# Flamingo block with a selective scan and a top-2 factorised FFN: delta times u moved from GpSimd to VectorE, with smaller edits to the gates

## The reference

```python
x_ = einsum('ed,bld->bel', in_proj_w, ctx)              # 512 channels
u = silu(conv4(x_) + conv_b)
dt_lo, Bm, Cm = split(einsum('ke,bel->bkl', x_proj_w, u))
delta = softplus(dt_proj_w @ dt_lo + dt_proj_b)
for t in range(512):                                    # 16 states for each channel
    state = state * exp(delta[t] * A) + (delta[t] * u[t]) * B[t]
    y[t] = sum_n state * C[t]
x = x + tanh(g_xattn) * (y + D * u) * silu(layernorm(x))
h = layernorm(x)
sc = h @ Wr.T; idx = top_k(sc, 2)
g = softmax(sc) * one_hot(idx); g = g / (g.sum() + 1e-8)
out = einsum('bts,btsr,srh->bth', g, h @ U, V)
gate = g @ sigmoid(attr @ Wa)
x = x + tanh(g_ffn) * out * (0.9 + 0.2 * gate)
```

## Time and profile before

| what | value |
|---|---|
| three runs | 554.56, 556.52, 556.17 us, median 556.17 |
| profiled execution | 554.37 us, its span 552.6 us |
| mean granted TensorE clock in it | 0.978 of full |
| DMA | 37.82 MB, mean 68 GB/s |
| length of the phases in it | phase 0 29.4, 1 and 2 24, 3 and 4 29, 5 to 11 28 to 34, 12 to 18 about 19, 19 13 us |
| before phase 0, after phase 19 | 32.3 us, 26.3 us |

### The profile page before, as it was taken

How to read it: one execution, slowest core, us unless ns; L and a number is a source line. 1 busy time by engine, 2 the same in 40 slices (tenths; PEclk the granted TensorE clock), 3 DMA queues, 4 the chain that set the end, 5 groups by cost and what they waited for, 6 DMA issues and landing times.

```text
span 552.6 us, 9388 instructions
## 1 busy us (share of the span) xinstructions
PE 502.3 (91%) x3154; PEld 381.2 (69%) x3154; DVE 459.9 (83%) x844; ACT 395.3 (72%) x704; POOL 479.3 (87%) x359
## 2 busy tenths in 40 slices
PE   6668989898798899999999999999899999999788
PEld 2156979767677687759687887678667756676654
DVE  2878999969899989779899999787878878977952
ACT  3369687758776787577968787578789778777632
POOL 0169999999999999989999999989999999988920
PEclk9877999999989999999999999999999999999899
DMA  4793000127320001046220000066100000000001
GB/s 109 258 351 142 2 2 0 39 54 240 131 77 2 0 1 58 0 159 211 77 95 2 20 1 21 6 226 222 49 20 1 21 20 21 1 20 21 0 21 38
DMA packets 18274, 37.82 MB, mean 68 GB/s; under 512 B 5537, under 2 KB 6305, under 8 KB 18226
## 3 DMA queue, kind: packets, MB, share of 16 engines
q1 hardware_dynamic: 18226, 37.22, 20.3%
HBM read 32.75 MB, written 4.46 MB: 67 GB/s over the span
## 4 chain that ended last, share of the span: by engine, by line
PE 52%; POOL 15%; ACT 13%; DVE 10%; issue 8%; DMA 1%; DVEq 0%; ACTq 0%; SPq 0%; POOLq 0%
PE p_s L718 14%; PE p_y L740 12%; POOL state L541 8%; PE p_v L773 5%; PE p_f L764 5%; DVE state L1197 4%; POOL dbu L526 4%; PE p_tr L684 4%; ACT da L960 3%; PE p_pr L647 3%; DVE x L1145 2%; PE p_pr L640 2%; ACT p_s L960 2%; ACT L912 2%; ACT L960 1%
## 5 line engine op out<-in xcount | busy, mean ns | idle before, releaser
L541 POOL TENSOR_TENSOR state<-state,c_bc 128x1024 f32<-128x1024 f32 (+1 forms) x158 | 304.5, 1940 | 14.0 <-DVE state L1197 11.2
L1197 DVE TENSOR_TENSOR_SCAN state<-da,p_s 128x512 f32<-128x512 f32 (+1 forms) x158 | 172.7, 1104 | 28.7 <-PE p_s L718 27.3
L718 PEld LDWEIGHTS p_s<-pair_b,du_t 128*128 128x128 f32 x1264 | 163.9, 196 | 36.1 <-issue 22.6
L718 PE MATMUL p_s<-pair_b,du_t 128*128 128x128 f32 x1264 | 178.9, 283 | 4.0 <-DVE state L1197 2.5
L740 PE MATMUL p_y<-ident,state 128*128 128x128 f32 x1024 | 150.4, 275 | 0.8 <-POOL state L541 0.8
L960 ACT ACTIVATE da<-delta,a_neg 128x512 f32<-128x512 f32 (+1 forms) x190 | 119.2, 642 | 25.2 <-DVE state L1197 24.7
L740 PEld LDWEIGHTS p_y<-ident,state 128*128 128x128 f32 x1024 | 120.6, 142 | 20.2 <-issue 15.3
L526 POOL TENSOR_TENSOR dbu<-du,pair_b 128x1024 f32<-128x1024 f32 (+1 forms) x64 | 116.5, 1820 | 4.7 <-DMA pair_b<-bc_rows 4.7
L1197 DVE TENSOR_TENSOR_SCAN state<-p_s,dbu 128x512 f32<-128x512 f32 (+1 forms) x98 | 101.1, 1037 | 5.5 <-POOL dbu L526 4.5
L960 ACT ACTIVATE p_s<-delta,a_neg 128x512 f32<-128x512 f32 (+1 forms) x130 | 74.9, 580 | 39.4 <-DVE state L1197 38.7
L764 PE MATMUL p_f<-u_sb,h_t 128*128 128x512 f32 x112 | 55.2, 595 | 1.5 <-DVE gw L1298 1.5
(11 more groups left out here) (178 smaller groups left out, 612.9 us busy)
## 6 DMA issues: line engine op xcount, KB each, us to landing
c_bc<-bc_rows SPq DMA_DIRECT2D x32, 512.0 KB, 5.6
pair_b<-bc_rows SPq DMA_DIRECT2D x13, 512.0 KB, 6.4
xs<-in_x SPq DMA_DIRECT2D x16, 256.0 KB, 4.3
out<-ot SPq DMA_DIRECT2D x14, 256.0 KB, 2.0
cx<-in_ctx_t SPq DMA_DIRECT2D x4, 512.0 KB, 3.6
u_sb<-in_u_w SPq DMA_DIRECT2D x1, 1024.0 KB, 7.9
v_sb<-in_v_w SPq DMA_DIRECT2D x1, 1024.0 KB, 14.6
w_in<-in_in_w_t SPq DMA_DIRECT2D x1, 384.0 KB, 4.5
```

The lines of the kernel that those rows point to most:

```text
L541: eng.tensor_tensor(pair, pair, c_bc[:, 2 * p:2 * p + 2, c0:c0 + w], ALU.mult).then_inc(po_cs, 1)
L718: mm = eng.matmul(p_s[g % BANKS][:, t * P:(t + 1) * P], du_t[:, f % 2, t, :], diagonals_of(n // 2)[:, n % 2, c0 // P + t, :], start=(t == ...
L1197: eng.tensor_tensor_scan(slot(g)[:, 0:w], decayed, added, first, ALU.mult, ALU.add).then_inc(ve_scan, 1)
```

## The change

`du` gets two buffers and is made by DVE for all phases: for phase f+1 after scan 9 of phase f, behind `gate_y(f - 1, 1)`. POOL no longer makes it. The waits of all readers become one on `ve_du`. The ring of `u` has five places in place of six. The casts of the two best indices go; the comparisons read the uint32 index as their scalar. In the gates, `0.2 * tanh(g_ffn)` is folded into `aw` and `0.9 * tanh(g_ffn)` into `gf` once, in phase 0, and one tiny operation of each tile goes.

```diff
-U_RING = 6
+U_RING = 5
-        du = sb("du", [P, L])
+        du = sb("du", [P, 2, L])
-        top_f = sb("top_f", [P, Q, 2])
-        GOPS = 9
-        def wait_for_du(eng, f):
-            if f:
-                eng.wait_ge(po_du, f)
-            else:
-                eng.wait_ge(ve_du, 1)
+        GOPS = 8
...
-            def times_u(f):
-                b, k, c0, w = PHASE[f]
-                eng.wait_ge(ve_dl, f + 1)
-                eng.wait_ge(pe_turn, TURN["du", f - 1] + 1)
-                eng.wait_ge(po_dbu, by_pool[f, pool_pairs(b)[0]])
-                if f == 1:
-                    eng.wait_ge(ve_dbu, 2)
-                eng.tensor_tensor(du[:, 0:w], delta[:, f % 2, 0:w], u[:, (Q * b + k) % U_RING, c0:c0 + w],
-                                  ALU.mult).then_inc(po_du, 1)
...
                 if p == pool_pairs(b)[0]:
-                    wait_for_du(eng, f)
-                eng.tensor_tensor(dbu[:, i % 2, :, 0:w], du[:, 0:w].unsqueeze(1).to_broadcast([P, 2, w]),
+                    eng.wait_ge(ve_du, f + 1)
+                eng.tensor_tensor(dbu[:, i % 2, :, 0:w], du[:, f % 2, 0:w].unsqueeze(1).to_broadcast([P, 2, w]),
                                   rows_of_b(p)[:, :, c0:c0 + w], ALU.mult).then_inc(po_dbu, 1)
...
-                early_u = k == 0 and c0 == 0
-                if early_u and not many:
-                    times_u(f + 1)
                 times_c(f, 3)
                 if many:
                     times_b(f, pairs[3])
-                if f < LAST and not (early_u and not many):
-                    times_u(f + 1)
                 times_c(f, 4)
...
             def turn_du(f):
-                wait_for_du(eng, f)
-                turn("du", f, du[:, :], PHASE[f][3] // P)
+                eng.wait_ge(ve_du, f + 1)
+                turn("du", f, du[:, f % 2, :], PHASE[f][3] // P)
...
             def exp_scores(T):
-                eng.wait_ge(ve_top, 4 * T + 4)
+                eng.wait_ge(ve_top, 3 * T + 3)
...
+            def times_u(f):
+                b, k, c0, w = PHASE[f]
+                eng.wait_ge(ve_dl, f + 1)
+                if f >= 2:
+                    eng.wait_ge(pe_turn, TURN["du", f - 2] + 1)
+                    eng.wait_ge(po_dbu, by_pool[f - 1, pool_pairs(PHASE[f - 1][0])[0]])
+                eng.tensor_tensor(du[:, f % 2, 0:w], delta[:, f % 2, 0:w], u[:, (Q * b + k) % U_RING, c0:c0 + w],
+                                  ALU.mult).then_inc(ve_du, 1)
...
-                else:
-                    eng.wait_ge(ve_top, 4 * T + 3)
-                    eng.tensor_copy(top_f[:, i, 0:1], top_i[:, i, 0:1])
-                    eng.tensor_copy(top_f[:, i, 1:2], top_i[:, i, 1:2]).then_inc(ve_top, 1)
...
-                    eng.scalar_tensor_tensor(out=e1, in0=iota_f[:, :], scalar=top_f[:, i, 0:1], in1=ex,
+                    eng.scalar_tensor_tensor(out=e1, in0=iota_f[:, :], scalar=top_i[:, i, 0:1], in1=ex,
                                              op0=ALU.is_equal, op1=ALU.mult).then_inc(ve_g, 1)
-                    eng.scalar_tensor_tensor(out=e2[:, i, :], in0=iota_f[:, :], scalar=top_f[:, i, 1:2], in1=ex,
+                    eng.scalar_tensor_tensor(out=e2[:, i, :], in0=iota_f[:, :], scalar=top_i[:, i, 1:2], in1=ex,
                                              op0=ALU.is_equal, op1=ALU.mult).then_inc(ve_g, 1)
...
                 elif part == 3:
                     made(6)
-                    eng.tensor_scalar(a[:, 4:5], a[:, 3:4], a[:, 2:3], 0.2, ALU.mult, ALU.mult).then_inc(ve_g, 1)
-                elif part == 4:
+                    eng.tensor_scalar(a[:, 4:5], a[:, 3:4], a[:, 2:3], gf[:, :], ALU.mult, ALU.add).then_inc(ve_g, 1)
+                else:
                     made(7)
-                    eng.tensor_scalar(a[:, 5:6], a[:, 4:5], 0.9, a[:, 2:3], ALU.add, ALU.mult).then_inc(ve_g, 1)
-                else:
-                    made(8)
-                    eng.tensor_scalar(gw[:, i, :], em, a[:, 5:6], gf[:, :], ALU.mult, ALU.mult).then_inc(ve_g, 1)
+                    eng.tensor_scalar(gw[:, i, :], em, a[:, 4:5], a[:, 2:3], ALU.mult, ALU.mult).then_inc(ve_g, 1)
...
                         eng.reciprocal(aw[:, :], aw[:, :]).then_inc(ve_k, 1)
                         eng.wait_ge(ve_k, 6)
+                        eng.tensor_scalar(aw[:, :], aw[:, :], gf[:, :], 0.2, ALU.mult, ALU.mult).then_inc(ve_k, 1)
+                        eng.wait_ge(ve_k, 7)
+                        eng.tensor_scalar(gf[:, :], gf[:, :], 0.9, None, ALU.mult).then_inc(ve_k, 1)
+                        eng.wait_ge(ve_k, 8)
...
-                    if n == 3 and mid >= 0:
-                        best_two(mid, 2)
...
                     if n == 9 and f:
                         gate_y(f - 1, 1)
+                    if n == 9 and f < LAST:
+                        times_u(f + 1)
```

More of the change, by code:

```diff
@@ L275, in flamingo @@
         po_dbu = sem("pool_dbu")
-        po_du = sem("pool_du")
         po_carry = sem("pool_state_carried")
@@ L1160, in combine @@
                     eng.wait_ge(ac_da, NS * (f - 1))
-                    wait_for_du(eng, f - 2)
+                    eng.wait_ge(ve_du, f - 1)
                 eng.scalar_tensor_tensor(out=delta[:, f % 2, 0:w], in0=p_pr[:, 0:w], scalar=0.0, in1=vsp[:, 0:w],
                                          op0=ALU.max, op1=ALU.add).then_inc(ve_dl, 1)
+            def times_u(f):
[6 more added lines that the diff above has]
+                                  ALU.mult).then_inc(ve_du, 1)
             def z_statistics(q):
@@ L1201, in first_dbu @@
                     eng.wait_ge(s_bbc[0], 16)
-                eng.tensor_tensor(dbu[:, 1, n, :], du[:, :], rows_of_b(0)[:, n, :], ALU.mult).then_inc(ve_dbu, 1)
+                eng.tensor_tensor(dbu[:, 1, n, :], du[:, 0, :], rows_of_b(0)[:, n, :], ALU.mult).then_inc(ve_dbu, 1)
             def times_c(f, p):
@@ L1255, in best_two @@
                     eng.max(top[:, i, :], sc).then_inc(ve_top, 1)
-                elif part == 1:
-                    eng.wait_ge(ve_top, 4 * T + 1)
+                else:
+                    eng.wait_ge(ve_top, 3 * T + 1)
                     if T >= Q:
@@ L1333, in _ @@
             combine(0)
-            eng.wait_ge(ve_dl, 1)
-            eng.tensor_tensor(du[:, :], delta[:, 0, :], u[:, 0, :], ALU.mult).then_inc(ve_du, 1)
+            times_u(0)
             eng.wait_ge(ve_du, 1)
@@ L1367, in _ @@
                         gates(mid, 4)
-                        gates(mid, 5)
                     if n == 7 and f < LAST:
@@ L1414, in _ @@
             f_statistics(15, 2)
-            for part in range(3):
+            for part in range(2):
                 best_two(14, part)
-            for part in range(6):
+            for part in range(5):
                 gates(14, part)
-            for part in range(3):
+            for part in range(2):
                 best_two(15, part)
             gate_hu(14)
-            for part in range(6):
+            for part in range(5):
                 gates(15, part)
```

## The result

The changed kernel took 580.17 us (median of 4, 575.68 to 583.83) against 555.44 us before (4 runs): a ratio of **1.046**, 95% interval 1.043 to 1.049. It is 25 us slower. The forecast was 553.6 us, its range ended at 557.2. The profiled execution took 575.68 us.

The account below looks back on a forecast made before the run. Bound by stretch: POOL from 118 to 191.5 and 258 to 290 us, mostly PE elsewhere. Terms +0.5 +0.9 -2.0 -0.8 -0.4 = -1.8 us against 555.4 gave 553.6 us; range 551.5 to 556.0, eight in ten 549.3 to 557.2.

Parts of the forecast that it names:

- part 2: du made on DVE beside busy POOL: 512 columns cost DVE 0.76 us and POOL 0.44, half for 256 columns.
- part 4: Two folded constants on DVE in phase 0, on the path ahead of phase 1's delta: +0.5 us (0.4 to 1.0).
- POOL's relief: du leaving POOL: -2.0 us between 118 and 191.5 us, -0.8 between 258 and 290, -0.4 between 378 and 526.
- DVE's load: Added DVE work: +0.6 us in phase 1, +0.3 in phase 2; also limits the 118 to 191.5 gain to -2.0 from -2.9.
- The second rival: DVE becomes the bound, scan 10 of each phase up to 0.76 us late: +3.2 us, 558.6 us; chance 0.12.
- the integer scalar: Comparisons reading the uint32 index as scalar: no change taken, between 0.1 us less and 0.2 more each.
- the new waits of `times_u`: DVE's new waits for making du are all on old events, so none of them delays it.
- the ring of five: u in five places: silu_u(f+5) needs skip(f) of ACT, six steps earlier in the same phase; costs nothing.
- phase 1 grew: Phase 1, where DVE had 0.1 us of slack: +0.6 us out of du's 0.76.
- part 5: New waits and u's ring: none delays an engine; POOL needs du only after its pair 4 product, DVE done earlier.

Follow-up runs that it names:

- b1: Kernel before plus one unread DVE product per phase, p_pr * vsp (one input in PSUM), du still by POOL: 559.6 us, ratio 1.008.
- b2: Kernel before plus one unread DVE product per phase, vsp * vsp (both inputs in SBUF), du still by POOL: 570.6 us, ratio 1.023.
- b3: Kernel before plus one unread DVE tensor_scalar per phase, 2 * vsp (single float32 SBUF input), du still by POOL: 567.6 us, ratio 1.020.
- r1: Kernel before, u in a ring of five, product delta * u left out from phase 1 on, readers take delta: 554.4 us, ratio 1.000.
- r2: r1 plus one unread DVE product per phase, p_pr * vsp (one input in PSUM): 559.8 us, ratio 1.011 to the kernel before.
- r3: r1 plus one unread DVE product per phase, vsp * vsp (both inputs in SBUF): 570.2 us, ratio 1.028 to the kernel before.
- e7: Kernel before with ring of five, no casts, integer index scalars, folded constants made by ACT; du still by POOL: 554.9 us, ratio 1.001.
- e4_split: Changed kernel with POOL's products with C of pairs 2 to 5 cut in two in full phases: 574.8 us, ratio 1.036 to the kernel before.
- e2_du_only: Kernel before with only du moved to DVE, in two buffers, and u in a ring of five: 574.3 us, ratio 1.032.
- e5_hold: Changed kernel with POOL waiting for du before its product with C of pair 4: 567.7 us, ratio 1.023 to the kernel before.

## Why the prediction was wrong

- **The price of du on DVE** (part 2) is the term that failed most. I took 0.76 us; the twelve full ones measured 2.54, the short ones 1.21 against 0.38. I read the earlier trace rows as a slowing by a fifth. It was a wait of 0.30 us for the rest of a POOL product and then 0.54 us of work: the POOL product beside it had only 0.30 us to go. An earlier start beside one of the products of 2.36 us would have given up to 2.9. The 1717 ns in the same rows belong to the POOL product behind that one, held while DVE worked; as the price of a du for POOL, the 0.44 us taken from it were right. I took one sample of a wait as a price.
- A second row was there and I read past it. `L1349`, a 32-column operation in phase 0, took 1.06 us in the trace of before:

```profile
45.15 1.06 DVE L1349 TENSOR_SCALAR aw<-aw 128x32 f32<-128x32 f32 x1
...
43.82 4.65 POOL L541 TENSOR_TENSOR state<-state,c_bc 128x1024 f32<-128x1024 f32 x2
```

  Its work is under 0.2 us; it ended as POOL's first product did. For the constants (part 4) this would have given up to 2 us in place of 0.5; they took 2.0.
- The Trainium skill (SBUF — State Buffer, "Who interferes with whom" and "SBUF: two separate sides") gives the rule that I needed and did not weigh: the pair of ports that DVE and GpSimd share is an exclusive lock, held for a whole instruction, and the other side fully blocks. It names both forms, DVE instructions with two SBUF inputs and the two-port modes of `tensor_scalar`. The runs agree (b1 at 693 ns at most, b2 up to 2640, b3 up to 4529). I quoted only the one line that says "contention", and gave it the price of slower work. The page has it that whoever comes first gets the pair; the 6.75 and 7.2 us show further that a DVE instruction that waits is not always next.
- **POOL's relief** (stretches 118 to 191.5, 258 to 290 and 378 to 526, -3.2 us together) was worth nothing, by r1. Busy for 99% of a phase and on the chain did not mean limiting: the chain names one of several ways of nearly the same length, and with POOL's work gone POOL waited 18 us more for DVE's scans. That the twelve `state` slots take up POOL's lag is likely, but no run tests it.
- **DVE's load** (+0.9 in phases 1 and 2, and 0.9 off the gain between 118 and 191.5) was too low. b1, 11.4 us of added DVE work that is never held, cost 5 us; r2 5.0. Against r1, phases 1 and 2 of r2 took 1.2 us more, near the +0.9. But phases 0, 3 and 4 took 2.4 us more, where I had nothing for phase 0 and took the other two to be paced by POOL. With the 36.3 us that DVE waits for PE I argued that DVE has slack; it has little in these phases.
- The sum of the parts: 0 for the relief, about +5 for load, about +2 for the small edits, and the rest of the 25, some 18 us, by the hold. This last figure is a remainder and not measured by itself; it fits the time that DVE spent held. 40.1 us in du are 28.7 more than its own work of 11.4, and some 6 of these lie in the short phases, which hardly grew. In b2 and r3, 11.7 and 8.9 us held cost 11.0 and 10.4.
- The second rival had the right side and place (scan 10, phases 0 to 2 without slack), but +3.2 us, as it used the same 0.76 for du. What I had as its evidence against, 36.3 us of waits for PE, fell to 28.1 only.
- Right: the integer scalar costs nothing (249 ns against 254), DVE never stood still at the new waits of `times_u`, the ring of five costs nothing (it is in r1 and e7), du costs POOL about 0.44 us, phase 1 grew (by 1.2 us, where I had 0.6). Of part 5, POOL's wait for du came out otherwise: 2.1 us, behind the three du that were held longest.

## What to carry to other kernels

Before work goes from POOL to DVE, look at where its inputs lie: beside a busy POOL, a DVE product with two SBUF inputs, or a float32 `tensor_scalar` from SBUF (of 32 columns or more, as measured here), costs the rest of POOL's running instruction and sometimes several more. One input in PSUM avoids it, if the bank can be spared. And test whether an engine that is 99% busy and on the chain limits at all, by leaving its work out, before paying for its relief elsewhere.

## What was not expected of the hardware

- The hold is for the length of whole POOL instructions: where a du started within a POOL instruction and got in at its end, it took the rest of that instruction plus 0.55 us for 512 columns and 0.28 for 256; the held 32-column products and sums of phase 0 took the rest plus about 0.04. A `tensor_scalar` of one column was not held (0.15 us), nor was the RECIPROCAL of 32 columns (0.35 us).
- A held DVE instruction may miss one to four changes of POOL from one instruction to the next: 2.9, 4.1 and 6.8 us in the changed kernel, 7.2 us in e4_split, 8.9 us in the profiled execution of e2_du_only. The traces have twelve such cases (three in the changed kernel, five in e2_du_only, two in e4_split, one each in e5_hold and b3_one), and in all twelve DVE got in only when POOL stood on a semaphore: none that had missed the first change got in at a later one. What decides whether the first is missed stays open; no run separates it.
- The POOL instruction behind the one that DVE waited for starts on time and is then longer by 0.44 to 0.49 us for a du of 512 columns (2.36 to about 2.83), and by 0.19 for one of 256 (1.27 to 1.46): some 0.1 us less than DVE's work.
